# Another order inside the steps of stage one: value product early, numerators behind one query tile, the queries' transposes in bank T0

## What is computed

```python
# per chunk c of x (8 chunks of 512 x 128); stage one
xn   = layernorm(x)
qkv  = xn @ Wqkv.T + bqkv                       # 4 tiles of 128 rows, 384 wide
q, k = rope(rmsnorm(q)), rope(rmsnorm(k))
qf, kf = relu(q), relu(k)
vk   = einsum('hlp,hld->hpd', [v, 1], kf)       # value product, per head
attn = (vk @ qf)[:-1] / (vk @ qf)[-1]           # numerators and denominators
out  = rmsnorm(attn @ Wout.T + bout)
ffn  = mx_quantize(xn) @ mx_quantize(W).T + b   # fp6 values, blocks of 32
x    = x + out + ffn
qkv2 = layernorm(x) @ [Wq2, Wk2, Wv2, Wgate].T + b   # "L1 tiles", 400 wide
# stage two: attention over the 8 chunks, routing, 16 experts and a shared one
```

## Time and profile before

| | us |
|---|---|
| median of 3 runs | 407.75 (403.55 to 407.75) |
| the profiled execution, as timed | 408.82 |
| its span, first to last instruction | 405.9 |
| stage one in it (until the last L1 tile is copied) | about 172 |
| VectorE busy | 342.2 (84% of the span) |
| TensorE busy | 325.6 (80%) |
| GpSimd busy | 236.5 (58%) |
| ScalarE busy | 187.4 (46%) |

### The profile page before, as it was taken

The page is one execution under the profiler, slowest core; times in us unless marked ns, Lnnn a source line. Parts: engine busy times, 40 slices in busy tenths (PEclk is TensorE's granted clock), DMA queues, the critical chain, the costliest instruction groups (busy, mean ns, idle before and its releaser), DMA issues.

```text
span 405.9 us, 5042 instructions
## 1 busy us (share of the span) xinstructions
PE 325.6 (80%) x1455; PEld 238.8 (59%) x1455; DVE 342.2 (84%) x846; ACT 187.4 (46%) x502; POOL 236.5 (58%) x157
## 2 busy tenths in 40 slices
PE   0179889889889875706029999999999999999995
PEld 0047667868768675704016666666666666666662
DVE  4875889797876765599999899999999999999891
...
DMA packets 13248, 12.49 MB, mean 31 GB/s; under 512 B 1549, under 2 KB 9925, under 8 KB 13221
## 3 DMA queue, kind: packets, MB, share of 16 engines
...
q0 software_dynamic: 736, 0.95, 1.1%
...
## 4 chain that ended last, share of the span: by engine, by line
PE 53%; DVE 25%; issue 7%; POOL 6%; ACT 5%; DMA 1%; ACTq 1%; POOLq 0%; DVEq 0%
PE Q L838 18%; PE VK L838 15%; PE T L838 9%; PE ND L838 7%; POOL prod_qk L778 3%; POOL prod_pv L788 2%; DVE rope_a L1248 2%; DVE rope_b L1250 2%; PE T L834 2%; PE Q L834 2%; DMA headmask<-in_c_headsel 1%; DVE attn L1280 1%; DVE chosen L1414 1%; DVE scr L1344 1%; DVE den L1277 1%
## 5 line engine op out<-in xcount | busy, mean ns | idle before, releaser
L788 POOL TENSOR_TENSOR prod_pv<-prob,qkv 128x1024 f32<-128x1024 f32 x32 | 69.6, 2212 | 45.0 <-DVE att L1361 24.2
L689 ACT ACTIVATE sg<-Q 128x512 f32<-128x512 f32 x72 | 43.1, 598 | 97.7 <-PE Q L838 94.9
L778 POOL TENSOR_TENSOR prod_qk<-qkv 128x1024 f32<-128x1024 f32 x32 | 75.9, 2397 | 16.7 <-DVE scr L1344 16.7
L838 PE MATMUL VK<-hid,w 128*128 128x512 f32 x144 | 74.5, 599 | 0.0
L838 PE MATMUL Q<-xT_hi,w_hi 128*128 128x512 f32 x72 | 52.3, 727 | 0.7 <-ACT combT L675 0.7
L1444 DVE TENSOR_TENSOR sgc<-ND,sg 128x512 f32<-128x512 f32 x64 | 43.7, 683 | 6.7 <-PE ND L838 4.6
L1457 DVE TENSOR_TENSOR hid<-T,sgc 128x512 f32<-128x512 f32 x64 | 43.6, 682 | 0.3
L838 PE MATMUL T<-xT_hi,w_hi 128*128 128x512 f32 x72 | 28.8, 401 | 17.1 <-DVE hid L1457 17.1
L838 PE MATMUL Q<-bias,ones 128*128 128x400 f32 (+1 forms) x64 | 29.7, 464 | 14.3 <-DVE xTs_lo L1299 9.2
L1344 DVE TENSOR_REDUCE scr<-prod_qk 128x128 f32<-128x1024 f32 x32 | 38.5, 1208 | 0.0
L1361 DVE TENSOR_REDUCE att<-prod_pv 128x128 f32<-128x1024 f32 x32 | 38.3, 1198 | 0.0
...
## 6 DMA issues: line engine op xcount, KB each, us to landing
...
```

The lines of the kernel that those rows point to most:

```text
L689: act.activation(sg[:, side(half, s), :], QB[side(half, s)][:, :], ACT.Silu).then_inc(sg_ready, 1)
L778: pool.tensor_tensor(prod_qk[:, t % 2], bc(qkv2[:, TH * half + t, j, 0:D], 1, NB), qkv2[:, :, j, D:2 * D], ALU.mult).then_inc(qk_prod, 1)
L788: pool.tensor_tensor(prod_pv[:, t % 2].rearrange("p (h e) b -> p b h e", e=HD), bc(prob[:, t], 3, HD), qkv2[:, :, j, 2 * D:QKV].rearrange( ...
L838: return pe.matmul(o, lhsT, rhs, start=start, stop=stop)
```

## The change

Only the order inside `step(i)` of TensorE, VectorE and ScalarE is changed, and a bank. TensorE: L1 tile 2 goes ahead of the FFN product, the queries' transposes and the value product come right behind the transposes of xd, L1 tile 3 and QKV tile 0 behind these, the numerators follow QKV tile 0, and QKV tiles 2 and 3 are spread over the output product and L1 tile 0. The queries' transposes go to bank T0, so `qf_transposes` waits for the copy of xnT, `attn_transposes` for that of qfT and `xn2_transposes` for that of xdT. VectorE and ScalarE follow that order. GpSimd's and SyncE's code is as before.

```diff
--- before.py
+++ after.py
@@ -563,7 +563,7 @@
 
             def qfT_evac(c):
                 act.wait_ge(qfT_ps, c + 1)
-                act.activation(qfT[:, :, :], tiles(T1), ACT.Relu).then_inc(qfT_ready, 1)
+                act.activation(qfT[:, :, :], tiles(T0), ACT.Relu).then_inc(qfT_ready, 1)
 
             def attnT_evac(c):
                 evac(attnT[:, :, :], tiles(T0), (attnT_ps, c + 1), [], attnT_ready)
@@ -607,31 +607,31 @@
 
             def step(i):
 
+                run(i, 1, xnT_evac)
                 norms_rooted(i)
                 weights_of_step(i)
-                run(i, 1, xnT_evac)
+                run_next(i, 5, l1_tile(2))
                 run(i, 2, xdT_evac)
-                run_next(i, 5, l1_tile(2))
                 act.wait_ge(rsqrt_step, RSQ * (i + 1))
                 run(i, 4, xn2_tiles(0))
+                run(i, 2, qfT_evac)
                 run(i, 4, xn2_tiles(1))
                 run_next(i, 5, l1_tile(3))
-                run(i, 2, qfT_evac)
                 if i == 0:
                     xn_tiles(0)
                 run(i, 1, qkv_tile(0))
-                run(i, 1, qkv_tile(1))
                 if i > 0:
                     run(i, 0, xn_tiles)
                 run(i, 4, xn2T_hi_evac)
-                run(i, 1, qkv_tile(2))
                 run(i, 2, attnT_evac)
+                run(i, 1, qkv_tile(1))
                 if i == STEPS - 2:
                     high_part(w3_hi[:, :], wraw[:, :], ld_w3, 32, w3_hi_ready)
                     return
+                run(i, 2, out_squares)
+                run(i, 4, l1_tile(0))
+                run(i, 1, qkv_tile(2))
                 run(i, 1, qkv_tile(3))
-                run(i, 4, l1_tile(0))
-                run(i, 2, out_squares)
                 run(i, 4, l1_tile(1))
                 run_end(i, 4, l1_tile(2))
                 run_end(i, 4, l1_tile(3))
@@ -873,8 +873,8 @@
 
             def qf_transposes(c):
                 pe.wait_ge(rope_sum, 2 * c + 2)
-                pe.wait_ge(xdT_ready, c + 1)
-                transposes(T1, lambda j: rope_ab[:, j, 0, :], signal=qfT_ps)
+                pe.wait_ge(xnT_ready, upto(c + 2))
+                transposes(T0, lambda j: rope_ab[:, j, 0, :], signal=qfT_ps)
 
             def value_product(c):
 
@@ -887,7 +887,7 @@
             def xn2_transposes(i):
                 def part(c):
                     pe.wait_ge(xn2_ready, 2 * c + 2)
-                    pe.wait_ge(qfT_ready, upto(i - 1))
+                    pe.wait_ge(xdT_ready, upto(i - 1))
                     transposes(T1, lambda j: xn2[:, j, :], signal=xn2T_ps)
                 return part
 
@@ -916,7 +916,7 @@
                 def part(c):
                     pe.wait_ge(attn_ready, c + 1)
 
-                    pe.wait_ge(xnT_ready, upto(i))
+                    pe.wait_ge(qfT_ready, c + 1)
                     transposes(T0, lambda j: attn[:, j, :], signal=attnT_ps)
                 return part
 
@@ -959,21 +959,21 @@
 
             def step(i):
                 run(i, 1, xn_transposes)
+                run_next(i, 5, l1_tile(2))
                 run(i, 3, ffn_product)
                 run(i, 2, xd_transposes)
-                run_next(i, 5, l1_tile(2))
+                run(i, 2, qf_transposes)
+                run(i, 2, value_product)
+                run_next(i, 5, l1_tile(3))
                 run(i, 1, qkv_tile(0))
-                run(i, 2, qf_transposes)
-                run_next(i, 5, l1_tile(3))
+                run(i, 2, numerators)
                 run(i, 1, qkv_tile(1))
-                run(i, 2, value_product)
                 run(i, 4, xn2_transposes(i))
-                run(i, 2, numerators)
+                run(i, 2, attn_transposes(i))
                 run(i, 1, qkv_tile(2))
+                run(i, 2, output_product)
+                run(i, 4, l1_tile(0))
                 run(i, 1, qkv_tile(3))
-                run(i, 2, attn_transposes(i))
-                run(i, 4, l1_tile(0))
-                run(i, 2, output_product)
                 run(i, 4, l1_tile(1))
                 run_end(i, 4, l1_tile(2))
                 run_end(i, 4, l1_tile(3))
@@ -1311,25 +1311,26 @@
                 run(i, 3, projection_scaled)
                 if at(i, 3):
                     vu_scaled(k_l0)
+                run(i, 2, head_blocks)
+                run(i, 3, plus_ffn)
                 run(i, 1, mx_scales)
                 if at(i, 4):
                     dve.wait_ge(wl1_scaled, 1)
                     low_part(wl1_lo[:, :], w_l1[:, :], wl1_hi[:, :], wl1_hi_ready, wl1_ready)
-                run(i, 2, head_blocks)
-                run(i, 3, plus_ffn)
                 if at(i, STEPS - 3):
                     low_part(w1_lo[:, :], wraw[:, :], w1_hi[:, :], w1_hi_ready, w1_ready)
                 run(i, 1, rope_tile(0))
+                run(i, -1, stats(0, stats1_ready))
+                run(i, 2, attention)
                 run(i, 1, rope_tile(1))
                 run(i, 1, mx_magic)
-                run(i, 2, attention)
+                run(i, 3, stats(1, stats2_ready))
+                run(i, 4, xn2T_lo_part)
                 run(i, 1, rope_tile(2))
-                run(i, 1, rope_tile(3))
-                run(i, 4, xn2T_lo_part)
-                run(i, -1, stats(0, stats1_ready))
-                run(i, 3, stats(1, stats2_ready))
                 if before_last(i):
                     ln_values(i)
+                run(i, 1, rope_tile(3))
+                if before_last(i):
                     rms_values(i)
                 if at(i, 1):
                     vu_sum()
```

## The result

The changed kernel takes 409.54 us (median of 8 runs, 407.33 to 410.4), the kernel before 406.13 us beside it: a ratio of 1.0072, interval 1.0036 to 1.0107. The profiled execution has a span of 407.9 us against 405.9. VectorE's busy time hardly moves (342.7 us against 342.2); TensorE's grows from 325.6 to 331.6 us with as many instructions. What moves above all is who waits. From here on "the change" is that kernel.

A forecast was written before the change was run, and what follows sets the result against it. Not VectorE's work alone but its waits, chiefly 2.20 us before vk_bd for TensorE's late value product, were taken to hold full steps. -0.5 + 1.8 + 0 + 1.0 = +2.3 us on 407.75 gave 410.0 us; 8 in 10: 404.5 to 414.5.

The forecast's parts named there:

- case A: Whole kernel: the forecast itself, 410.0 us, own range 407 to 412 us; chance 62%.
- Head of the step, -1.75 us: Full step: early value product brings vk_bd 4.25 us behind L1111 instead of 6.00, gaining 1.75 us.
- New waits: Full step: waits at L1111, the root, QKV tile 0, numerators and last rotary tile take up the 1.75 us gain.
- A full step, 15.8: Steps 5 to 8: 15.8 us a step against 15.9, -0.5 us over four.
- Steps 1 to 4, +1.8: Pipeline fill: GpSimd's loop grows as the magic pair stands behind statistics and attention; L1111 of step 4 at 77.2, +1.8 us.
- Bank T0, 0: The queries' transposes in T0 instead of T1 cost nothing, since T0 is copied out long before.
- Step 9, 0: Tail: attention 0.4 us earlier, but L1 tile 0 behind the output product; the four L1 tiles end about as late, 0.
- Step 10 and what hangs on it, +1.0: Tail: statistics, needing GpSimd's x, precede the low part, which starts at 161.1 instead of 160.08; L1 tiles follow, +1.0 us.
- Sum +2.3 on the span: Whole kernel: -0.5 + 1.8 + 0 + 1.0 = +2.3 us, added to the 407.75 us median.
- Rival B: Full steps: new waits don't arise, VectorE is the bound, 14.1 us a step, 403.4 us in all; chance 16%.
- C: Full steps: TensorE falls to half clock, +2.9 us a step; two such steps 415.8 us, four 421.6; chance 12%.
- D: Steps 2 to 4: their loss does not come, the change does nothing that is seen, 407.5 us; chance 10%.

The follow-up runs named there:

- experiment 6: The change with L1 tile 2 put back behind the transposes of xd, its copy behind that of xdT: 405.93 us, ratio 1.0005.
- Experiment 2: The change with the low part of xn2T ahead of the statistics on VectorE in the last two steps: 407.79 us, ratio 1.0047.
- experiment 4: The kernel before with only the queries' transposes moved to bank T0, with the change's three waits: 404.67 us, ratio 0.9963.
- kernel 12: kernel 10 with L1 tile 3 behind the numerators, its copy behind xn_tiles, and plus_ffn ahead of head_blocks: 394.77 us, ratio 0.9726.
- kernel 10: The kernel before with value product and qfT copy early, and the low part ahead of the last rotary tile: 397.03 us, ratio 0.9793.
- kernel 11: kernel 10 with numerators, attention and magic pair early, attnT's copy ahead of QKV tile 1's squares, QKV tile 3 later, plus_ffn ahead of head_blocks: 408.91 us, ratio 1.0093.
- experiment 5: The change with VectorE's order of before, only the low part staying ahead of the last rotary tile: 433.97 us, ratio 1.0698.
- 3: The change with the magic pair ahead of attention and the second rotary tile on VectorE in steps 2 and 3: 408.47 us, ratio 1.0062.
- 9: The change with L1 tile 2 behind the transposes of xd, plus the magic pair ahead of attention in all steps: 410.8 us, ratio 1.0136.

## Why the prediction was right, and what it did not see

The forecast, 410.0 us and no change that can be told by 1%, came out (409.54), and by case A. That 410.0 and 409.54 lie so close is luck in part: the forecast starts from a median of 407.75 us, where eight runs of the kernel before give 406.13, and adds 2.3 us, where the medians differ by 3.4; the two errors cancel. Its steps one by one:

- **Head of the step, -1.75 us: right in kind, measured -1.57** (vk_bd 4.43 us behind L1111 instead of 4.25). TensorE went on 1.30 us behind the last rotary tile, as walked, after a wait of 0.88 us; experiment 6 showed that this wait is worth 0.31 us of step.
- **New waits: right.** All named waits are there: L1111 0.88 (about 1.0), square root 0.21 (0.3), QKV tile 0 0.27 (0.4), numerators 0.94 in steps 7 and 8 (0.3 with the statistics ahead of them, measured 0.15 in step 6), last rotary tile 0.49 (0.3). What the wait before L1111 replaces was misread for half the steps: 0.47 us in steps 5 and 6, but 1.72 in steps 7 and 8.
- **A full step, 15.8: measured 15.56.** The path was right. Counted from the end of the last rotary tile, vk_bd came at 5.31 us (walked: 5.21), the end of the numerators at 8.51 (8.60), that of the low part at 12.91 (13.15), that of QKV tile 3 at 14.79 (15.0). Small excesses, rounding among them, add up: four full steps gave -1.4 us instead of -0.5, and the 15.56 lies just under the 15.6 to 16.0 that were named as a sign.
- **Steps 1 to 4, +1.8: measured +1.75 at the start of L1111, with two errors that cancel.** The magic pair of step 4 ended at 72.42 us (forecast 72.1) and L1111 started at 77.33 (77.2). But from the pair of step 2 to that of step 3 it was 15.0 us (forecast 15.5), and on to that of step 4 16.1 (15.2), since TensorE stood at half clock behind its idle 1.79 and 0.70 us, which makes the value product 1.1 us longer (2.25 us); the text had taken full clock there. The +1.75 is that of two executions: experiments 2 and 4, which have the change's order and the old order in these steps, give 76.46 - 75.02 = +1.44. That the root operations wait for the sums on GpSimd was right: L1120 takes 0.42 us at 47.17 and at 62.20, and ends within 0.04 us of the second sum.
- **Bank T0, 0: right**, experiment 4.
- **Step 9, 0: measured -0.4. Step 10 and what hangs on it, +1.0: measured +2.1.** L1111 of step 10 comes 0.62 us later than before and the last copy 2.67; 0.7 us of this does not show in the span. The mechanism (low part behind the statistics) was right, and its size too: the L1 tiles of chunk 7 start 1.11 us later (169.59 against 168.48). What the text did not have is that these four then take 4.78 us to the last copy instead of 3.22, most of them at half clock. Experiment 2 moves the copy back.
- **Sum +2.3 on the span: measured +2.0**, on the medians +3.4.

Rival B (VectorE becomes the bound, 14.1 us a step) did not come in the change, but its number is met by kernel 12 with 13.9: the room was there, and the change's order does not use it. C (half clock in full steps) did not come; half clock came in the steps around them. D is refuted by step 4; its 407.5 us does not follow from its own terms either, which give 407.75 - 0.5 + 1.0 = 408.25.

So the full step came out for the reason that the prediction gave: the value product comes sooner, and the chain behind it, which ends with low part, L1 tile 0, QKV tile 3, last rotary tile and ScalarE's last tile, takes most of the gain back. What the prediction did not do is ask which pieces of the change earn and which cost. The value product alone, with its copy and the low part in the right places, brings 2.1% (kernel 10); L1 tile 2 at the head costs 0.31 us a full step (6); the tail costs in the profile (2). The middle, with numerators and attention ahead of QKV tile 1, loses in kernel 11, where it stands with the magic pair ahead of attention: the squares of tile 1 come late and QKV tile 3 waits for its bank. Kernel 12 gets the numerators sooner without passing QKV tile 1 and gains 2.3 us. That the bank is to blame in the change as well is not shown, and its full step speaks against it: there the bank was free 1.65 us before QKV tile 3 took it. My own next theories missed twice more: I blamed VectorE's order (experiment 5, +7%) and the late magic pair (3 and 9). What stays open: what the middle costs in the change, with the magic pair behind attention; what the half clock in the steps around the full ones costs by itself; and the split between tail and the rest, for which the intervals are too wide.
